# A decoder layer's kernel: Mamba units of 1024 columns, layer norms' normalising, first tap, values' copies and a square on ScalarE, and gate kernel rows added up once

## The reference

```python
x = x + mamba(_layernorm(x), ...)           # in-projection, 4-tap convolution, silu, step sizes, scan over 128 steps
x = x + mlstm(_layernorm(x), ctx, ctx, ...) # 4 heads, stabilised gates, norm per head
x = x + graph(_layernorm(x), ...)           # 6 nodes, each an 8-head attention of earlier nodes; ends in a layer norm
# the scan of the first block, for 512 channels and 16 states:
h = dA_t * h + dBu_t;  y = einsum(h, Cm) + u * D;  y = y * silu(gate)
# the gates of the second block: q is the normed x, k and v are both the context
gate_in = concatenate([q, k, v]);  ig = gate_in @ igate_kernel;  fg = gate_in @ fgate_kernel
```

## Time and profile before

| what | value |
|---|---|
| median of the 3 runs | 1309.74 us (1309.69 to 1315.06) |
| the profiled execution, its own time | 1308.01 us |
| its span, from the first to the last instruction | 1306.2 us |
| busy: PE, DVE, ACT | 1098.0, 1053.6, 720.6 us |

### The profile page before, as it was taken

How to read it: one execution, slowest core, us unless ns; L and a number is a source line. 1 busy time by engine, 2 the same in 40 slices (tenths; PEclk the granted TensorE clock), 3 DMA queues, 4 the chain that set the end, 5 groups by cost and what they waited for, 6 DMA issues and landing times. The chain is left out here.

```text
span 1306.2 us, 27811 instructions
## 1 busy us (share of the span) xinstructions
PE 1098.0 (84%) x11504; PEld 822.0 (63%) x11504; DVE 1053.6 (81%) x1683; ACT 720.6 (55%) x1692; POOL 2.9 (0%) x10
## 2 busy tenths in 40 slices
PE   3845668988999899989988998899888988897886
PEld 2723445766676667666666666666666666676665
DVE  2289887799999999999999999999999889725112
ACT  1434532576657665776567556755576646444332
POOL 0000000000000000000000000000000000000000
PEclk9767775999999999999999999999999989999998
DMA  6440343004100410030112211030104000000000
GB/s 190 122 178 32 107 153 113 33 3 130 41 26 33 132 42 25 34 105 28 50 49 62 71 50 49 16 117 33 58 3 130 33 25 34 2 1 10 2 1 9
DMA packets 53710, 76.14 MB, mean 58 GB/s; under 512 B 15376, under 2 KB 38672, under 8 KB 53456
## 3 DMA queue, kind: packets, MB, share of 16 engines
q1 hardware_dynamic: 53584, 74.37, 17.9%
HBM read 63.60 MB, written 10.75 MB: 57 GB/s over the span
## 5 line engine op out<-in xcount | busy, mean ns | idle before, releaser
L979 DVE TENSOR_TENSOR_SCAN unit_buf<-dec,unit_buf 128x512 f32<-128x512 f32 x256 | 311.9, 1218 | 11.7 <-ACT dec L753 11.0
L753 ACT ACTIVATE dec<-dts,a_neg 128x254 f32<-128x254 f32 x512 | 225.6, 499 | 42.5 <-DVE unit_buf L979 37.3
L972 DVE TENSOR_TENSOR unit_buf<-dtus,bs 128x512 f32<-128x512 f32 x256 | 175.0, 686 | 6.3 <-DMA dtus<-dt_rows 2.5
L990 DVE TENSOR_TENSOR unit_buf<-unit_buf,cs 128x512 f32<-128x512 f32 x256 | 175.3, 685 | 0.5
L1087 DVE TENSOR_REDUCE mx<-heads 128x16 f32<-128x2048 f32 x48 | 109.2, 2276 | 50.1 <-PE heads L602 50.0
L487 PE MATMUL ps<-unit_buf,fold 128*32 128x256 f32 x1024 | 89.0, 420 | 52.4 <-DVE unit_buf L990 52.3
L825 ACT ACTIVATE pr<-heads 128x512 f32<-128x512 f32 x192 | 99.1, 603 | 49.0 <-PE heads L617 49.0
L571 PE MATMUL ps<-node,wq_f 128*128 128x256 f32 x384 | 93.6, 387 | 7.8 <-ACT node L840 7.8
L640 PE MATMUL heads<-node,we_f 128*128 128x256 f32 x384 | 94.7, 389 | 0.0
L647 PE MATMUL heads<-aT,wo_f 128*128 128x256 f32 x384 | 93.7, 387 | 0.9 <-DVE aT L1096 0.9
L581 PE MATMUL heads<-wv_f,node 128*128 128x256 f32 x384 | 91.8, 382 | 0.0
(11 more groups left out here) (178 smaller groups left out, 1777.8 us busy)
## 6 DMA issues: line engine op xcount, KB each, us to landing
dts<-dt_rows SPq DMA_DIRECT2D x32, 512.0 KB, 3.8
dtus<-dt_rows SPq DMA_DIRECT2D x32, 512.0 KB, 5.2
node<-in_w_edgeT SPq DMA_DIRECT2D x18, 256.0 KB, 3.6
dt_rows<-dt SPq DMA_DIRECT2D x32, 128.0 KB, 2.4
dt_rows<-th SPq DMA_DIRECT2D x32, 128.0 KB, 2.5
bs<-bc_rows SPq DMA_DIRECT2D x32, 128.0 KB, 4.6
cs<-bc_rows SPq DMA_DIRECT2D x32, 128.0 KB, 4.3
xin<-in_x SPq DMA_DIRECT2D x8, 256.0 KB, 6.2
```

The costliest lines, as they stand in the source:

```text
L753: last = fn(dec[k % 2][:, a, :, 1:L], dts[c % 2][:, blk, :].rearrange("p (b t) -> p b t", b=GB)[:, :, 1:L], ACT.Exp, scale=a_neg[:, c, blk ...
L972: v.tensor_tensor(inf[k % 2][:], dtus[c % 2][:, 2 * pair:2 * pair + 2, :], bs[:, q:q + 1, :].broadcast_to([P, 2, T]), ALU.mult).then_inc(s ...
L979: v.tensor_tensor_scan(hst[k % 2][:].rearrange("p a b -> p (a b)"), dec[k % 2][:].rearrange("p a b t -> p (a b t)"), inf[k % 2][:].rearran ...
L990: v.tensor_tensor(prd[(i * UNITS + k) % PRDS][:], hst[k % 2][:], cs[:, q:q + 1, :].broadcast_to([P, 2, T]), ALU.mult).then_inc(sig["outflo ...
```

## The change

- A unit is all 4 blocks, 1024 columns: 16 units a group, each with its own sum. Feed, scan and weigh work in place in one of 3 buffers (`ring`), and the feed waits until PE has summed the unit that used the buffer before. The order within a unit is weigh of the last, feed of the next, scan.
- `normalise` on ACT: after the logarithm and exponential two instructions multiply the (negated) means by the root, and two of 256 columns write the rows. DVE keeps the statistics and negates the means. All four norms.
- The tap that reads the projection unshifted, with the bias, is computed by ACT straight from PSUM; DVE keeps the other three.
- The copies of the values of each head, and the square in the norm per head, go to ACT. DVE no longer multiplies the values by the reciprocal first; it works with unnormalised values and puts the reciprocal into the variance by three tiny operations.
- The gate kernels' rows for k and v, which meet the same context, are added once; PE then has 4 products of 256 columns per group in place of 6.
- All four tables are written anew.

```diff
-CUNITS = NGRP * BLKS // 2
+CUNITS = NGRP
 UNITS = IC * CUNITS
-PRDS = 5
...
-    if _k >= 2 and _k % 2 == 0:
-        U_STEPS += [("u", "add", _k // 2 - 1)]
+    if _k >= 1:
+        U_STEPS += [("u", "add", _k - 1)]
...
-X_AT = [18, 38, 43, 44, 47, 48, 49, 51, 53, 54, 55, 57, 58, 60, 63, 65]
...
+X_AT = [37, 38, 43, 44, 48, 48, 50, 53, 54, 55, 56, 57, 58, 60, 64, 65]
...
-        dec = [sb(f"dec{j}", [P, 2, GB, L]) for j in range(2)]
-        unit_buf = sb("unit_buf", [P, 4 + PRDS, 2 * T])
-        inf, hst, prd = ([unit_buf[:, j].rearrange("p (a n) -> p a n", a=2) for j in slots]
-                         for slots in ((0, 1), (2, 3), range(4, 4 + PRDS)))
+        dec = [sb(f"dec{j}", [P, BLKS, GB, L]) for j in range(2)]
+        ring = [sb(f"ring{j}", [P, BLKS, T]) for j in range(RING)]
...
-
-                c, q = j // NGRP, j % NGRP
...
                 if q == 0:
                     after(pe, "y_read", i, c)
-                after(pe, "outflow", i, 2 * j + 2)
-                for k in (2 * j, 2 * j + 1):
-                    for a in range(2):
-                        r0 = SD * (k % 2 * 2 + a)
-                        last = mm(MY[r0:r0 + SD, 0:T], fold[:], prd[(i * UNITS + k) % PRDS][:, a, :],
-                                  start=(q == 0), stop=(q == NGRP - 1), tile_position=(0, r0))
+                after(pe, "outflow", i, k + 1)
+                for blk in range(BLKS):
+                    last = mm(MY[SD * blk:SD * (blk + 1), 0:T], fold[:], ring[(i * UNITS + k) % RING][:, blk, :],
+                              start=(q == 0), stop=(q == NGRP - 1), tile_position=(0, SD * blk))
...
-                    for k in range(3 * HC):
+                    if i == 0:
+                        pe.wait_ge(sig["gate_sum"], 1)
+                    for k in range(2 * HC):
                         src = mqT if k < HC else ctxT
                         last = mm(MB[0:GROWS, 0:T], wgate[:, k, :], src[:, k % HC, :],
-                                  start=(k == 0), stop=(k == 3 * HC - 1))
...
+            def normalise(chain, n, i, src, mean_var, inv, dst):
+
+                rstd_of(chain, f"ln_var{n}", f"ln_rstd{n}", i, inv[:])
+                after(act, f"ln_rstd{n}", i, 1)
+                for b in range(GB):
+                    m = chain.mark(fn(mean_var[:, b, 0:1], mean_var[:, b, 0:1], ACT.Copy, scale=inv[:, b:b + 1]))
+                chain.wait(m)
+                for b in range(GB):
+                    last = fn(dst[:, b, :], src(b), ACT.Identity, scale=inv[:, b:b + 1], bias=mean_var[:, b, 0:1])
+                return last
+
...
-                    rstd_of(a_chain, "ln_var1", "ln_rstd1", i, rstd[:])
+                    after(act, "dtu_stored", i - 1, 16 * BLKS)
+                    normalise(a_chain, 1, i, lambda b: xin[:, b, :], mv, rstd, rows).then_inc(sig["ln1_rows"], 1)
...
-                        last = fn(hs_pad[:, 2 * j + a, :, 1:L + 1],
-                                  MA[:, a * T:(a + 1) * T].rearrange("p (b t) -> p b t", b=GB), ACT.Copy)
+                        fn(hs_pad[:, 2 * j + a, :, 1:L + 1],
+                           MA[:, a * T:(a + 1) * T].rearrange("p (b t) -> p b t", b=GB), ACT.Copy)
+                    after(act, "y_ready", i - 2, IC)
+                    for a in range(2):
+                        c = 2 * j + a
+                        last = fn(u[p][:, c, :], MA[:, a * T:(a + 1) * T], ACT.Identity,
+                                  scale=convh[:, 5 + c * 4:6 + c * 4], bias=convh[:, c:c + 1])
                     last.then_inc(sig["inproj_read"], 1)
...
                     after(act, f"dt_in{c % 2}", i, 16 * (c // 2 + 1))
                 after(act, "state", i, k - 1)
-                for a in range(2):
-                    blk = 2 * pair + a
-                    last = fn(dec[k % 2][:, a, :, 1:L],
+                for blk in range(BLKS):
+                    last = fn(dec[k % 2][:, blk, :, 1:L],
                               dts[c % 2][:, blk, :].rearrange("p (b t) -> p b t", b=GB)[:, :, 1:L], ACT.Exp,
...
+                after(act, "h_ps", i, h + 1)
+                fn(hrow[:, :, h, :], MB[:, 0:GB * XP].rearrange("p (b d) -> p b d", b=GB), ACT.Copy
+                   ).then_inc(sig["h_read"], 1)
+
             def head_norm(i, _):
+                after(act, "hcentre", i, 1)
+                fn(hsq, hn, ACT.Square).then_inc(sig["hsquare"], 1)
                 rstd_of(m_chain, "hvar", "hrstd", i, hva[:])
 
             def mlstm_out(i, step):
                 if step == 0:
...
                     a_chain.start(i)
                     after(dve, "x_loaded", i, 16)
...
-                    layer_norm(i, a_chain, 1, lambda b: xin[:, b, :], mv, bn, rstd, LN_EPS, rows).then_inc(sig["ln1_rows"], 1)
+                    after(dve, "ln1_rows", i - 1, 1)
+                    layer_norm(i, a_chain, 1, lambda b: xin[:, b, :], mv, bn, rstd, LN_EPS)
                 if step == 4:
 
                     after(dve, "inproj_read", i, 2)
-                    marks = [a_chain.mark(v.tensor_scalar(u[p][:, c, :].rearrange("p (b t) -> p b t", b=GB),
-                                                          hs_pad[:, c, :, 0:L], convh[:, 4 + c * 4:5 + c * 4],
-                                                          convh[:, c:c + 1], ALU.mult, ALU.add)) for c in range(IC)]
-                    for k in range(1, 4):
+                    marks = [0] * IC
+                    for k in (0, 2, 3):
...
+                if c == 0:
                     after(dve, f"bs_in{q}", i, 16)
-                after(dve, "state", i, k - 1)
-                v.tensor_tensor(inf[k % 2][:], dtus[c % 2][:, 2 * pair:2 * pair + 2, :],
-                                bs[:, q:q + 1, :].broadcast_to([P, 2, T]), ALU.mult).then_inc(sig["inflow"], 1)
+                after(dve, "ysum", i, k - RING + 1)
+                v.tensor_tensor(ring[(i * UNITS + k) % RING][:], dtus[c % 2][:],
+                                bs[:, q:q + 1, :].broadcast_to([P, BLKS, T]), ALU.mult).then_inc(sig["inflow"], 1)
 
             def scan(i, k):
+                states = ring[(i * UNITS + k) % RING][:].rearrange("p k t -> p (k t)")
                 after(dve, "decay", i, k + 1)
                 after(dve, "inflow", i, k + 1)
-                after(dve, "outflow", i, k - 1)
-                v.tensor_tensor_scan(hst[k % 2][:].rearrange("p a b -> p (a b)"),
-                                     dec[k % 2][:].rearrange("p a b t -> p (a b t)"),
-                                     inf[k % 2][:].rearrange("p a b -> p (a b)"), 0.0, ALU.mult,
+                v.tensor_tensor_scan(states, dec[k % 2][:].rearrange("p k b t -> p (k b t)"), states, 0.0, ALU.mult,
                                      ALU.add).then_inc(sig["state"], 1)
 
             def weigh(i, k):
-                c, q = k // CUNITS, k % CUNITS // 2
+                c, q = k // CUNITS, k % CUNITS
+                states = ring[(i * UNITS + k) % RING]
                 after(dve, "state", i, k + 1)
-                after(dve, "ysum", i, (k - PRDS) // 2 + 1)
-                if c == 0 and k % 2 == 0:
+                if c == 0:
                     after(dve, f"cs_in{q}", i, 16)
-                v.tensor_tensor(prd[(i * UNITS + k) % PRDS][:], hst[k % 2][:],
-                                cs[:, q:q + 1, :].broadcast_to([P, 2, T]), ALU.mult).then_inc(sig["outflow"], 1)
+                v.tensor_tensor(states[:], states[:], cs[:, q:q + 1, :].broadcast_to([P, BLKS, T]),
+                                ALU.mult).then_inc(sig["outflow"], 1)
 
             def gather(i, c):
...
                     feed(i, 0)
+                if k >= 1:
+                    weigh(i, k - 1)
                 if k + 1 < UNITS:
                     feed(i, k + 1)
-                if k >= 1:
-                    weigh(i, k - 1)
                 scan(i, k)
...
+                    if i == 0:
+                        dve.wait_ge(sig["const_loaded"], 16 * 5)
+                        v.tensor_tensor(wgate[:, HC:2 * HC, :], wgate[:, HC:2 * HC, :], wgate[:, 2 * HC:3 * HC, :],
+                                        ALU.add).then_inc(sig["gate_sum"], 1)
...
                 m_chain.link(v.tensor_scalar(hmu[:], hmu[:], 1.0 / XD, None, ALU.mult))
-                m_chain.link(v.tensor_tensor(hn, hn, hmu[:].unsqueeze(2).broadcast_to(wide), ALU.subtract))
-                m_chain.link(v.tensor_tensor(hsq, hn, hn, ALU.mult))
+                v.tensor_tensor(hn, hn, hmu[:].unsqueeze(2).broadcast_to(wide), ALU.subtract).then_inc(sig["hcentre"], 1)
+                after(dve, "hsquare", i, 1)
                 m_chain.link(v.tensor_reduce(hva[:], hsq, AX.X, ALU.add))
-                v.tensor_scalar(hva[:], hva[:], 1.0 / XD, HEAD_EPS, ALU.mult, ALU.add).then_inc(sig["hvar"], 1)
+                m_chain.link(v.scalar_tensor_tensor(hva[:], hva[:], 1.0 / XD, den[:], ALU.mult, ALU.mult))
+                m_chain.link(v.tensor_tensor(hva[:], hva[:], den[:], ALU.mult))
```

(17 more changed lines are left out.)

61 lines of the change are left out of this document (29 added, 32 removed).

## The result

The changed kernel takes 1323.73 us (median of 18, 1310.41 to 1331.58), the kernel before 1309.72 (18 runs, 1307.83 to 1315.06). The ratio is 1.0094, 95% interval 1.0076 to 1.0112: slower by 0.9%, where 1300 us and "faster" were forecast. The profiled execution of the changed kernel took 1329.22 us with a span of 1327.4, 5.5 above the median, so its trace shows more than the median loss. The longest of the 18, 1331.58, counts as a slow run and is left out of the ratio. The first things to see are the spread, 1310 to 1330 in the other 17 where the kernel before has 7 us, and the clock: TensorE's mean granted clock is 0.926 in the median run and 0.939 in the fastest (1310.41); the kernel before has 0.939 in its median run.

A forecast was written before the change was run, and what follows sets the result against it. VectorE was taken as fullest, TensorE close behind, handovers setting node 5. The span of 1306.2 less 8.5 at the start, six groups unchanged, plus 0.4 at the end gave 1298.1, so 1300 us; range 1265 to 1318.

The forecast's parts named there:

- The sum of a group: Steady group of six nodes: 137.1 us, as before; VectorE's gain of 2.4 given back at the group's end.
- node 5: The group's last node, set by a chain of handovers: from 22.9 to 25.1 us.
- node 3: Fourth node of a group: from 24.6 to 23.2 us, with fewer units and gates 0.9 shorter.
- node 4: Fifth node of a group: 24.0 us, against 23.9 before.
- Rival 1: VectorE's relief passes on: 4.7 us less in each of six groups, 1272 us; chance 0.27.
- rival 4: Ring of three buffers: feeds wait for TensorE's sums; priced at nothing, worst case 10 us a group as part of rival 2.
- norm 3: Third layer norm at the group's end: normalising on ScalarE takes 2.0 us instead of 1.2, delaying the next first matmul.
- norm 4: Fourth layer norm: VectorE waits about 2.0 us where wait and work took 1.5 before, 0.5 worse.
- The three delays of its first matmul: Node 5: attention products 1.3 us late, normalising 2.0 for 1.2, gate copy of 0.6 ahead; 2.5 in all.
- Rival 2: Slower through ScalarE's chain at the group's end: 2.4 us a group, 1314 us; chance 0.13.
- The start: Stretch before the first node's maximum: 8.5 us saved, between 3 and 13, from larger units and relieved VectorE.
- its 2.2 for the group's end: Delay of some 2.2 us remaining at the next maximum after node 5, counted once against the start's gain.

The follow-up runs named there:

- e5: Changed kernel with one table entry put back: the gates' tiny transposes ahead of node 5's keys on TensorE, as in the kernel before; 1310.9 us, ratio 1.0003.
- e9: Kernel before with one table entry moved the other way: the gates' tiny transposes behind node 5's keys on TensorE; 1327.7 us, ratio 1.0121.
- e13: Changed kernel, order untouched, with six unread products filling TensorE's 0.67 us wait between the gates' transposes and the first head; 1310.6 us, ratio 1.0013.
- e4: Changed kernel with one sum of a unit moved from before to behind the scores of node 2; 1325.2 us, ratio 1.0099.
- e10: Changed kernel with the gates' transposes back ahead of the keys and layer norms 3 and 4 normalised on VectorE again; 1306.1 us, ratio 0.9976.
- e14: e10 with six unread products in TensorE's 0.99 us wait in node 1, between the halves of the step size's projection; 1304.8 us, ratio 0.9970.
- e7: Changed kernel with all work ScalarE took over given back to VectorE; longer units, summed gate rows and new tables stay; 1382.4 us, ratio 1.0537.

## Why the prediction was wrong

**The sum of a group held.** An undisturbed group takes 137.0 us for the forecast 137.1, its nodes within 0.5 us each, and for the reasons given: nodes 1 and 2 are filled by VectorE, and node 5 is the chain (24.8 for 25.1). That the sum fits to 0.1 us is in part luck: node 3 came 0.5 shorter and node 4 0.5 longer. Rival 1 (the relief passes on) was rightly put below it, and rival 4 (the ring) rightly priced at nothing: between 386 and 1080 us feeds wait for sums 0.4 us in all. The parts of node 5 fit less well than their total: norm 3 costs 0.3 and not 0.8, norm 4 0.4 and not 0.5, and node 5 is still 24.2 with both norms on VectorE, 1.3 above the 22.9 before. The three delays of its first matmul also add up to 2.7 and not 2.5.

**The step that failed is the one that was not written.** I took the granted clock of 1.00 in a steady group for a property of the group, and went through each engine's order only for waits that last. The gates' transposes moved behind the keys add a wait of 0.67 us off the path, priced at nothing; without a fall it does cost 0.2 us or less. Its real price is that of the falls it brings: removing it (e5), bringing it in (e9) and filling it (e13) put it at 13, 18 and 13 us. That is 13 of the 23.7 us between 1300 and 1323.7, and the whole of the loss against the kernel before; the rest of the miss is mostly the start, below. Over the 18 runs of the changed kernel, time and lost clock go together: a run at 0.939 takes 1310.4, one at 0.920 takes 1329.8. With (1 - clock) x time as the lost time, 0.061 x 1310 = 80 and 0.080 x 1330 = 106, 19 us of time go with 26 us of lost clock. In its one run at the clock of the kernel before, the changed kernel takes the same time as that. Rival 2 had the sign right, but its mechanism (the two-operand instructions at 617 ns, queues in full) is not it: those instructions take 560 to 594 ns.

**The start was mis-sized.** Of -8.5 us, -0.6 came (-3.2 in e5). Up to the addition ahead of norm 2 the gain is 3.7 us (175.33 for 179.06), not the 10.7 that the forecast implied with its 2.2 for the group's end. From the traces: the first feed starts at 69.6 and not 67.6. In the first group the second projection waits 1.66 us for the first taps on ScalarE, in the kernel before 0.75 for the copies; but its eight products also take 3.78 us, at the lower clock, where they take 1.99 in the kernel before. The clock makes the difference: e4 and e13 have the same wait of 1.66 and products of 1.99, and their first feeds start at 66.9 and 67.7, their first maxima stand at 244.1 and 243.7. The second projection in the changed kernel, then in e13:

```profile
25.95 3.78 PE L449 MATMUL ps<-th,win 128*128 128x256 f32 x8 [1.66 <-ACT u L719]
```

```profile
25.88 1.99 PE L450 MATMUL ps<-th,win 128*128 128x256 f32 x8 [1.66 <-ACT u L726]
```

So a start without that fall saves 3.3 to 3.7 us, and about 5 of the 8.5 are missing for another reason. One part of it: the new table has 18 units ahead of that point (36 old ones) where the old has 35, one old unit or 2.5 us. From the last head's copy to the first maximum it takes 24.5 us for 22.1, which looks like the +2.2 of the group's end, but in e5 it is 23.0. This was read from the traces and not tried, and the rest of the missing 5 us stays open.

**The end.** The 11.9 us in the last two groups are above all three nodes of the seventh: node 4 with the long fall (30.8 for 22.0), node 2 with a shorter one (19.7 for 17.7), and node 5 (23.9 for 22.1, the clock 0.93 and 0.92). In e10 these two groups take 234.9, against 234.2 before.

## What to carry to other kernels

In this kernel, with TensorE busy nine tenths of the time, a wait of under a microsecond that costs nothing on the path cost 1 to 8 us through the clock each time a fall followed it. So compare the granted clock window by window before and after, and the spread of the run times with the mean clock, before looking for a longer path. When steps change their order, look for narrow products next to a wait on TensorE and put wide work over the wait, or fill it with products that nobody reads; then count the falls again, since they may turn up elsewhere (e14). With a larger unit of work on one engine, look at the short, urgent operations queued behind it (e7).
